# Expert one-hots spread over the tiles, a border without Pool, L0 decays by VectorE scans, and D times x added by VectorE

## What is computed

```python
# mixer, for every token t and head
dA    = exp(dt * A)
state = state * dA + dt * outer(x, B)        # a recurrence over t
y     = state @ C + D * x                    # D: one number for a head
y     = rmsnorm(y * silu(z)) @ W_out

# experts
scores = softmax(xt @ Wr)                    # (4096, 8)
G, idx = top_k(scores.T, 1024)               # for each expert
X_in   = xt[idx]
h      = gelu(X_in @ W1 + b1)
out[idx] += G[..., None] * (h @ W2 + b2)
```

## Time and profile before

| what | value |
|---|---|
| median of 3 runs | 1750.13 us (1749.46 to 1754.74) |
| the profiled execution's own time | 1762.29 us |
| its span, first to last instruction | 1760.2 us |
| PE busy | 1582.4 us (90%) |
| DVE busy | 1120.2 us (64%) |
| ACT, POOL busy | 768.2 us (44%), 710.1 us (40%) |
| mean granted PE clock | 0.935 of full |

### The profile page before, as it was taken

The page is one execution under the profiler, slowest core; times in us unless marked ns, Lnnn a source line. Parts: engine busy times, 40 slices in busy tenths (PEclk is TensorE's granted clock), DMA queues, the critical chain, the costliest instruction groups (busy, mean ns, idle before and its releaser), DMA issues.

```text
span 1760.2 us, 23296 instructions
## 1 busy us (share of the span) xinstructions
PE 1582.4 (90%) x7307; PEld 1092.0 (62%) x7307; DVE 1120.2 (64%) x2583; ACT 768.2 (44%) x1562; POOL 710.1 (40%) x751
## 2 busy tenths in 40 slices
PE   4989999999999999998878889999868988898896
PEld 3555756557575756656534555555557877787886
DVE  4767586676858577672388888788745445545442
ACT  1435162533426162441245555666445444444452
POOL 1456456263645536364012222323324342434242
PEclk8979999999999999998978899999979999999998
DMA  6000100101010010101141111111023233423222
GB/s 193 1 12 13 38 24 1 60 0 48 12 48 12 0 60 0 36 13 37 37 134 34 57 37 57 60 61 60 28 79 91 64 71 69 94 61 70 70 43 24
DMA packets 66855, 84.00 MB, mean 48 GB/s; under 512 B 12360, under 2 KB 57296, under 8 KB 66768
## 3 DMA queue, kind: packets, MB, share of 16 engines
q1 hardware_dynamic: 54480, 65.86, 11.4%
q0 software_dynamic: 12288, 17.05, 5.8%
HBM read 57.53 MB, written 25.36 MB: 47 GB/s over the span
## 4 chain that ended last, share of the span: by engine, by line
PE 25%; issue 13%; POOL 6%; DVE 5%; ACT 2%; another core or an unknown queue 1%; POOLq 1%; DMA 0%; DVEq 0%; ACTq 0%; SPq 0%
PE bank L2065 24%; POOL yb L921 2%; POOL Xs L913 2%; POOL ry L929 1%; PE bank L2448 1%; DVE OL L1864 1%; DVE am L1879 1%; ACT m0big L1318 1%; DVE EW L2005 1%; POOL ry L926 0%; POOLq L967 0%; DVE w2l L2016 0%; POOL out L978 0%; DVE hits L1783 0%
## 5 line engine op out<-in xcount | busy, mean ns | idle before, releaser
L2020 DVE TENSOR_TENSOR aml<-m0big,amh 128x512 fp32r<-128x512 f32 x128 | 87.9, 691 | 228.2 <-ACT amh L1323 213.9
L1318 ACT ACTIVATE m0big<-bank,eb 128x512 f32<-128x512 f32 x128 | 87.7, 685 | 218.9 <-PE bank L2065 192.1
L978 POOL DMA_INDIRECT out<-EW,IDX x64 | 111.6, 1744 | 160.4 <-DVE EW L2005 143.6
L2065 PE MATMUL bank<-w2h,amh 128*128 128x256 f32 x512 | 152.7, 298 | 0.0
L2065 PE MATMUL bank<-w2h,aml 128*128 128x256 f32 x512 | 148.5, 290 | 0.0
L2065 PE MATMUL bank<-w2l,amh 128*128 128x256 f32 x512 | 148.4, 290 | 0.0
L2065 PE MATMUL bank<-h2T,EW 128*128 128x512 f32 x320 | 146.7, 595 | 0.3
L2065 PEld LDWEIGHTS bank<-Xdt,E 128*128 128x128 f32 x768 | 95.4, 200 | 55.9 <-issue 55.9
L952 POOL DMA_INDIRECT xg<-rows_d,IDX x64 | 62.4, 975 | 142.0 <-DVE IDX L1872 90.2
L2065 PE MATMUL bank<-EW,am 128*128 128x256 f32 x512 | 115.8, 379 | 1.2 <-DVE am L1642 1.2
L2065 PE MATMUL bank<-xTh,w1h 128*128 128x512 f32 x256 | 104.9, 410 | 9.0 <-ACT m0big L1318 7.6
(11 more groups left out here) (327 smaller groups left out, 3851.7 us busy)
## 6 DMA issues: line engine op xcount, KB each, us to landing
EW<-in_e_w SPq DMA_DIRECT2D x16, 1024.0 KB, 5.7
m0big<-dA_d SPq DMA_DIRECT2D x16, 512.0 KB, 4.7
xin<-in_L_attn_x SPq DMA_DIRECT2D x8, 512.0 KB
xp<-in_L_attn_x SPq DMA_DIRECT2D x8, 512.0 KB, 3.7
rows_d<-xo SPq DMA_DIRECT2D x8, 512.0 KB, 3.0
x_d<-xb SPq DMA_DIRECT2D x8, 512.0 KB, 4.0
xnT_d<-nT SPq DMA_DIRECT2D x8, 512.0 KB, 4.4
out<-x SPq DMA_DIRECT2D x32, 128.0 KB, 1.7
```

The lines of the kernel that those rows point to most:

```text
L978: g.indirect_dma_start(out=out_rows, out_offset=bass.IndirectOffsetOnAxis(ap=IDX[:, 4 * u + c:4 * u + c + 1], axis=0), in_=ye[:, q, c, :], ...
L1318: a.activation(am2[:, j % 2, :], bank[j % 2][:, :], ACT.Gelu, bias=eb1[:, u // 2, j:j + 1]).then_inc(gelu_sig.sem, 1)
L2020: v.tensor_tensor(aml[:, j % 4, :], am2[:, j % 2, :], amh[:, j % 4, :], ALU.subtract).then_inc(am_low.sem, 1)
L2065: return t.matmul(out_, lhsT, rhs, start=first, stop=last)
```

## The change

It has four parts.

1. **L0 decays.** `terms`, `decay_sums`, ACT's `decays` and the mask Gm are gone. The log decays of a step are transposed once on PE (LOGT, in `decay_log_sums`, which is moved up behind the input projections), ACT takes their exponential into dAT0, SP stores this to DRAM (dA0_d) and loads each chunk's row broadcast to 128 partitions (512 KB, two buffers, four loads in a step). In `chunk` DVE makes both halves of E by scans against the identity row ID0 and multiplies them by B·C straight from PSUM. PE's B·C of the next chunk now waits for the previous chunk's products (signal M).
2. **D times x.** DVE adds XD to yb in `sums`, ahead of the wait for the intra-chunk part. Pool's `gated` is the gate product alone.
3. **L1 and the border.** `threshold` is called in tiles 0, 1 and 3 of the first five steps and not in tile 2; `above` to `slots` move from tiles 18, 19, 22, 23 to 22, 23, 24, 25; expert 0's one-hots are made 16 and 16 in tiles 27 and 28. Pool issues `gather(0)` before its last y_rms but two and leaves the meeting at `phase` (8 instead of 9); PE does `tokens(0)` before the meeting, and ACT and DVE start with the tokens and not with the weights.
4. **Expert one-hots.** DVE makes four one-hots at each j of an even unit, PE's `slots` reads 16 behind `up` 6 of the even unit and 16 behind `up` 1 of the odd one, `index` is at j = 3 of the odd unit, and Pool issues both gathers of the next expert in the odd unit behind a scatter.

```diff
-BUNCH = 11
+BUNCH = 16
...
+            def store_decays(i):
...
+                s0.dA.wait_ge(sp, i, 1)
...
+                sp.dma_start(dA0_d.rearrange("c (h t) -> (c h) t", t=P), dAT0[:, :]).then_inc(s0.dA_stored.sem, 16)
+
+            def load_decays0(i, c):
+
+                if c >= 2:
+                    s0.E.wait_ge(sp, i, 2 * (c - 1))
+                else:
+                    s0.dA_stored.wait_ge(sp, i, 16)
+                    s0.E.wait_ge(sp, i - 1, 2 * (c + 3))
+                sp.dma_start(dA0[c % 2][:, :], dA0_d[c].partition_broadcast(P)).then_inc(s0.dA_loaded[c % 2].sem, 16)
...
-            with sp.Fori(1, STEPS - 2) as b:
+            for b in range(1, STEPS - 2):
                 load_x(b + 2)
+                decays_of(b + 1)
                 load_residual(b + 1)
+                later_decays_of(b + 1)
                 store_back(b)
...
@@ Pool, gated
                 s.y0.wait_ge(pool, i, c + 1)
-                s.xd.wait_ge(pool, i, c + 1)
-                ch.put(g.tensor_tensor(yb[:, q, :], yb[:, q, :], XD[:, q, :], ALU.add))
-                ch.see(pool)
                 s.zs.wait_ge(pool, i, c + 1)
...
@@ Pool, end of L1
-            gather(0)
+                if n + 2 == TILES1:
+                    gather(0)
             y_rms1(STEPS - 1, CH - 1)
             gather(1)
-            pool.drain().then_inc(phase, 1)
-            pool.wait_ge(phase, 9)
...
             for u in range(UNITS):
-                if u % 2 == 0 and u:
+                if u:
                     scatter(u - 1)
-                if u + 2 < UNITS:
+                if u % 2 and u + 1 < UNITS:
+                    gather(u + 1)
                     gather(u + 2)
-                if u % 2:
-                    scatter(u - 1)
...
@@ ACT, decay_exp (now called behind conv_tanh 0 and raw 4)
+                s.dA_stored.wait_ge(act, i, 0)
+                a.activation(dAT0[:, 1:P], LOGT[:, 1:P], ACT.Exp).then_inc(s.dA.sem, 1)
...
@@ DVE, chunk and sums of L0
+                s.dA_loaded[q].wait_ge(dve, i, 16 * (c // 2 + 1))
+                s.intra_full.wait_ge(dve, i, c - 1)
+                for j in range(L.segs):
+                    v.tensor_tensor_scan(E[:, q, 512 * j:512 * (j + 1)], dA0[q][:, 512 * j:512 * (j + 1)], ID0, 0.0,
+                                         ALU.mult, ALU.add).then_inc(s.E.sem, 1)
                 s.g_full.wait_ge(dve, i, c + 1)
...
-                v.tensor_tensor(Gm[:, q, :], GP, triU[:, :], ALU.mult).then_inc(s.gm.sem, 1)
...
-                    v.tensor_tensor(e3, e3, Gm[:, q, :].unsqueeze(1).to_broadcast([P, 4, P]),
-                                    ALU.mult).then_inc(s.M.sem, 1)
+                    v.tensor_tensor(e3, e3, GP.unsqueeze(1).to_broadcast([P, 4, P]), ALU.mult).then_inc(s.M.sem, 1)
...
                 s.t1.wait_ge(dve, i, c + 1)
+                s.xd.wait_ge(dve, i, c + 1)
+                ch.put(v.tensor_tensor(yb[:, q, :], yb[:, q, :], XD[:, q, :], ALU.add))
+                ch.see(dve)
                 s.intra_full.wait_ge(dve, i, c + 1)
                 v.tensor_tensor(yb[:, q, :], yb[:, q, :], INTRA[:, :], ALU.add).then_inc(s.y0.sem, 1)
...
@@ DVE, L1 tile and expert unit
-                if n < 15:
-                    threshold(n)
+                if c != 2 and i < 5:
+                    threshold(3 * i + c - c // 3)
...
                         if j == 0:
                             high_onehots(e + 1)
-                        elif j < 7 and j % 2:
-                            onehots(e + 1, j // 2)
-                        elif j == 7:
-                            index(e + 1)
+                        for k in range(4):
+                            onehot(e + 1, 4 * j + k)
+                    elif q and e + 1 < NE and j == 3:
+                        index(e + 1)
...
@@ PE, chunk of L0
-                s.R.wait_ge(pe, i, c + 1)
-                decay_sums(0)
...
-                s.bs.wait_ge(pe, i, c)
+                s.M.wait_ge(pe, i, c * L.segs)
...
-                for j in range(1, L.segs):
-                    decay_sums(j)
...
@@ PE, border and expert unit
+            s1.t1.wait_ge(pe, STEPS, 0)
+            tokens(0)
+            pe.drain().then_inc(phase, 1)
+            pe.wait_ge(phase, 8)
...
-                    if u % 2 == 0 and u + 2 < UNITS and j > 2 and j % 2:
-                        slots(u // 2 + 1, (j - 3) // 2)
+                    if u % 2 == 0 and u + 2 < UNITS and j == 6:
+                        slots(u // 2 + 1, 0)
+                    elif u % 2 and u + 1 < UNITS and j == 1:
+                        slots(u // 2 + 1, 1)
```

More of the change, by code:

```diff
@@ L337, in program @@
         pool_prep = sem("pool_prep")
+        own = sem("identity_rows_ready")
         phase = sem("phase")
@@ L1718, in step0 @@
                     dveb.end()
+            v.tensor_copy(ID0.rearrange("p (h t) -> p h t", h=4),
+                          ident[:, :].unsqueeze(1).to_broadcast([P, 4, P])).then_inc(own, 1)
+            v.memset(dAT0[:, 0:1], 0.0).then_inc(own, 1)
+            dve.wait_ge(own, 2)
             norm(0)
@@ L2159, in chunk @@
                 n = L.state
[L2160 removed]
+                s.M.wait_ge(pe, i, c * L.segs)
                 if c == 0:
[L2162 to L2168 removed]
+                    s.dA.wait_ge(pe, i, 1)
                 mm(GP, s.u_buf[0:n, 4, cols(c)], s.Ct_buf[0:n, cols(c)])
                 t.transpose(BTP[:, 0:n], s.u_buf[0:n, 4, cols(c)], ident[0:n, 0:n]).then_inc(s.g_full.sem, 1)
[L2171 to L2172 removed]
             def recur(L, s, i, c):
@@ L2421, in _ @@
                     project1(*divmod(n - 1, CH))
-                if n == 19:
+                if n == 23:
                     ge = GE[:, :, :, :].rearrange("p a e t -> p (a e t)")
                     pe.wait_ge(ge_ready, 2)
-                    s1.xb.wait_ge(pe, 6, 0)
+                    s1.xb.wait_ge(pe, 7, 0)
                     mm(bank[2][:, :], triU[:, :], ge).then_inc(pre_full, 1)
                     mm(bank[3][:, :], ones[:, :], ge).then_inc(pre_full, 1)
-                elif n == 27:
+                elif n == 28:
                     s1.xb.wait_ge(pe, STEPS, 0)
                     slots(0, 0)
-                elif n in (28, 29):
-                    slots(0, n - 27)
+                elif n == 29:
+                    slots(0, 1)
             y_turned1(STEPS - 1, CH - 1)
             project1(STEPS - 1, CH - 1)
-            pe.drain().then_inc(phase, 1)
-            pe.wait_ge(phase, 9)
-            def parts(high, low):
-                return ((high[0], high[1]), (high[0], low[1]), (low[0], high[1]))
             def tokens(u):
@@ L2449, in tokens, with parts @@
                     last.then_inc(xt_full.sem, 1)
+            s1.t1.wait_ge(pe, STEPS, 0)
+            tokens(0)
+            pe.drain().then_inc(phase, 1)
+            pe.wait_ge(phase, 8)
+            def parts(high, low):
+                return ((high[0], high[1]), (high[0], low[1]), (low[0], high[1]))
             def up(u, j):
@@ L2482, in _ @@
             LAG = 3
-            tokens(0)
             for u in range(UNITS):
```

146 lines of the change are left out of this document (65 added, 81 removed).

## The result

The median went from 1751.84 us (20 runs, 1745.59 to 1755.51) to 1745.53 us (20 runs, 1735.47 to 1754.46): a ratio of 0.9961, 95% interval 0.9945 to 0.9976. That is 6.3 us faster (0.4%), where 50 were forecast, and outside the range of 1666 to 1730 us. The profiled execution of after took 1738.63 us (span 1736.8).

The account below looks back on a forecast made before the run. PE was taken to bound L0, with DVE's loop 1.3 us shorter and the bound after the change. L0 -15, border -8, L1 0 and experts -27 sum to -50: 1750.1 to 1700 us, range 1666 to 1730 us.

Parts of the forecast that it names:

- The step that failed: L0, B·C of chunk 1: PE's wait for chunk 0's products costs no more than PE gained in the first tile.
- the 15 us: L0: gain of 0.5 us a tile over 28 tiles, from PE's 12.47 to DVE's 11.95 us.
- rival 4: L0: gaps behind DVE lower PE's clock; some 5 of 28 tiles at 1.2 GHz eat all the gain; chance 0.06.
- The lock: L0: scans and Pool's products of SBUF tiles exclude each other; one scan per tile charged with 0.84 us more.
- The base of VectorE's sum: L0: DVE's earlier tile of 11.15 us, with changes of -0.03 in all, leaves its loop at 11.1 us.
- VectorE as the bound: L0: DVE's loop of 11.95 us (11.1 to 12.8) becomes longer than PE's 10.75 and sets the tile.
- The small prices: L0 per tile on DVE: scans 1.21 us each, products of E 0.687 each, XD addition +0.69, wait for ry -1.27.
- The D product: L0: adding XD on DVE costs +0.69 us a tile; Pool's addition of 1.27 us leaves the ry chain.
- The border: Between L1 and experts: PE's idle 10.30 us shrink to about 1.5, weights cost about 1; taken as -8 us.
- The experts: Expert stage: 30.6 us of one-hot gaps go, 3.5 us charged for gathers; -27 us.
- The new gap of 1.5 us at GELU of `up` 2: Experts, even units: PE waits 1.5 us because four one-hots delay DVE's low part, offsetting 1.5 us of clock gain each.
- the 0.5 us of late gathers in each odd unit: Experts: the gathers fit by 0.4 us; 0.5 us charged in each of seven odd units, 3.5 in all.

Follow-up runs that it names:

- run 7: Changed kernel with layer 0's 56 scans replaced by a one-column copy, so decays are left out of the intra-chunk part: 1629.0 us, ratio 0.9309 to the kernel before.
- run 6: Changed kernel with Pool's two products of a layer-0 chunk waiting until VectorE's two scans are done: 1681.0 us, ratio 0.9597 to the kernel before.
- run 3: Changed kernel with two unread PE matmuls added per layer-0 chunk ahead of the B·C product: 1703.0 us, ratio 0.9667 to the kernel before.
- run 12: Kernel before with only the addition of D times x moved from Pool to VectorE, decay sums kept on PE, no scans: 1739.2 us, ratio 0.9941.
- 1: Kernel before with only the layer-0 part of the change (scans and D times x on VectorE): 1807.4 us, ratio 1.0263.
- 2: Kernel before with everything of the change but the layer-0 part: 1695.9 us, ratio 0.9626.
- 8: Kernel before with the decays by scans alone, D times x still added by Pool: 1815.6 us, ratio 1.0362.
- run 9: Changed kernel with Pool's products waiting for the scans and one unread PE matmul per layer-0 chunk: 1661.0 us, ratio 0.9487 to the kernel before.
- run 5: Changed kernel with one unread PE matmul added per layer-0 chunk ahead of the B·C product: 1749.0 us, ratio 0.9996 to the kernel before.

## Why the prediction was wrong, point by point

- **The step that failed** is the price of PE's waits in L0, clock included. The prediction said of B·C of chunk 1 that "the 15 us assume that it costs no more than that", and against rival 4 that "the gaps that I expect are 1 to 3 us", as if gaps of this size left the clock alone. They came as expected, 2.29 and 1.45 us, and the clock fell to 0.53 for the next 13.5 us. Rival 4, with a chance of 0.06, is what happened in L0: 57.9 us of clock and 28.8 of idleness against 47.7 of saved work (run 7). My figure for it, some 5 tiles at the lower level, was about right in size: 57.9 us are six tiles of 9.5. That the kernel still came out faster is luck: the experts gave 27 us more than the sum had for them.
- **The lock** was sized right and judged wrong. I charged 0.84 us a tile; the rows give 0.82 (19.7 us in 24). I treated it as a term of VectorE's loop. Taking it away (run 6) gave 64 us and not 23. Yet even without it L0 gave little: the six steps of run 6 are 12 us shorter than before, where the sum without the lock had 1.37 x 24 = 33.
- **The base of VectorE's sum** was misread. The tile of 11.15 us in the earlier trace rows is not an average one. Its two products of E took 2.13 us together, and I took 2 x 1.479 off it:

```profile
481.14 2.13 DVE L1585 TENSOR_TENSOR E<-E,Gm 128x512 f32<-128x512 f32 x2
```

  With its own figure the tile is 0.8 us longer, 11.9 without the lock. And PE was not end to end there, as I had read it from one tile of the four:

```profile
489.83 0.63 PE L2196 MATMUL bank<-ident,yb 128*128 128x128 f32 x4 [0.78 <-DVE x L1621]
```

- **VectorE as the bound.** In after VectorE is busy 73.2 of 108.7 us a step, and in run 3 the same work (73.7 us) fits a step of 102.4. So a busy loop did not set the pace; the lateness of single results did (the products of chunk 0, then zs).
- **The small prices held:** scans 1.205 us undisturbed, the products of E 0.673 (forecast 0.687), the addition of XD 0.676 (0.69), the wait for ry shorter by 1.3. PE waited for the products of E six times in six steps, as forecast. The transfers of the decays appear in no wait of PE or VectorE.
- **The D product** was counted as +0.69 of work and -1.27 of wait in a loop that did not bind before. It gave 11.8 us by itself, in part since PE's wait for x, which I had at nothing, went with it (run 12).
- **The border** gave 10.0 us against 8. The gap in front of the tokens, for which I had left 1.5 us, is gone, and the one at the weights' low part is 2.82 us, where I had about 1.
- **The experts** gave 54 and not 27; the mechanism was right and the size off. The gap of 30.6 us went. The new gap of 1.5 us at GELU of `up` 2 and the 0.5 us of late gathers in each odd unit, 14 us in all, did not come: behind the wait for w1l at the border, PE waited 1.3 us for gathered rows in the whole stage and for nothing else that shows. And the gap had cost more than itself. PE's busy time in an even unit was 27.4 us and is 24.8, 2.6 each and 18 in seven, where I had 1.5 each (some 0.5 us of it are 16 `slots` matmuls that moved to the odd unit). Six of the odd units also went from 26.0 us to 24.8, or 25.5 in one, while unit 1 grew from 24.2 to 25.7; together the odd units gave 5 us. PE's waits for GELU (L1318), 7.6 us in sum before, are gone. Which of the edits removed them no run tells.
- **L1**: +0.6 us (the other 2.7 of the row are L0's eighth step), within the 5 that I allowed.

Shown by runs: that the loss is the L0 part's (1, 2), the scans' within it (8, 12), that PE's clock is most of it (3, 7, 9), and that the lock with Pool is the larger cause of the scans' cost (6). The window of six steps is 640 us in after, 589 without the lock and 551 without the scans. Left open: why 13 us are missing between the sum of runs 1 and 2 and after, and why the clock falls behind the same two gaps in some steps of runs 5 and 6 and not in others.

## What to carry to other kernels

Where PE bounds a stage with little room, ask of work taken off PE whether the engines behind it have more room than that: here gaps of 2.29 and 1.45 us in PE were followed by 13.5 us at about half the clock. Test a suspected clock loss with matmuls for nothing in front of the wait, as many as cover it. If the kernel gets faster, the gap and not the work was the price; if it doesn't, that proves little, since one matmul brought nothing in run 5 and two brought 42 to 51 us in run 3. Then look for the next wait along the stream. And before adding two-input work to VectorE, see what Pool does at that moment and let Pool wait, if its result isn't due yet; one wait was worth 64 us here, at no cost of work.

## What the runs showed of the hardware

- PE's granted clock fell behind short gaps: in all six steps of after behind about 2.3 and 1.4 us (PE busy 0.54 of 4.20 us in the step shown), in all six of run 5 behind a single wait of 2.1 to 2.2 us, and in four of six of run 6 behind 0.8 and 1.4 us. In the step shown it then stayed low for 13.5 us of full work. Behind single gaps of 1.2 us (run 6, six times) and 0.54 us (run 9) the matmuls that follow kept their full speed.
- The length of a gap alone does not decide: 0.57 and 1.31 us in run 5 were followed by the full clock in three steps and by the low one in three, and at the head of the steps of run 9 a wait of 0.6 to 0.7 us for xo was followed by a granted clock of 0.52 to 0.67.
- The Trainium skill, TensorE: Matmul & The Clock Gate, section A second HAM failure mode, describes a kernel whose PE idles briefly and often between groups of matmuls and so swings between the two clock levels; these traces agree, with 0.88 against 0.97 for the same 2304 instructions.
- A scan and a Pool product of SBUF tiles hold each other (two scans 3.13 us against 2.33, Pool's Xs 2.06 against 1.04), and so do Xdt's product and Pool's XD (1.39 us against 0.68). The product of E with an operand in PSUM showed no hold: 48 of them averaged 673 ns in after and 678 in run 6.
- 64 matmuls more that nobody reads (run 3) made the kernel 42 to 51 us faster. PE's busy time in the six steps of L0 fell in spite of them, from 594.1 us to 588.6, at a clock of 0.95 and not 0.88.
